# One kernel for a graph layer with attention and experts: edge totals by a running sum on VectorE, ranks between turned tiles, and the change behind the last step fetched earlier

## The reference, cut to what matters

```
xn = layernorm(x)
x  = x + gnn(xn, edges) + linear_attention(xn)
x  = x + experts(layernorm(x))
```

## Time and profile before

| | |
|---|---|
| median of 3 runs | 1640.06 us (1639.51 to 1644.37) |
| profiled execution | 1639.86 us |
| its span | 1637.8 us |
| TensorE busy | 1553.7 us |
| VectorE busy | 812.1 us |
| ScalarE busy | 335.5 us |
| GpSimd busy | 250.5 us |
| mean DMA rate | 100 GB/s |

### The profile page before, as it was taken

One profiled execution on the slowest core, in us unless ns is written; L12 is line 12 of the kernel. 1 busy time (PEld: TensorE's weight loads), 2 busy tenths in 40 slices (PEclk: granted clock), 3 DMA queues, 4 the chain that ended last, 5 costly groups with the idle time before them and its releaser, 6 DMA issues.

```text
span 1637.8 us, 21951 instructions
## 1 busy us (share of the span) xinstructions
PE 1553.7 (95%) x8501; PEld 1033.9 (63%) x8502; DVE 812.1 (50%) x1539; ACT 335.5 (20%) x493; POOL 250.5 (15%) x234
## 2 busy tenths in 40 slices
PE   6999999999899999999989999899999999999995
PEld 4566666557779999999887555444444444444442
DVE  7545447998877889994897333111111111111111
ACT  2321112001223245560372210100100000001000
POOL 1087820000000000000000027111111111111110
PEclk9999999999999999999989999999999999999998
DMA  9900010000004625313111327925629211613315
GB/s 273 334 2 1 2 61 1 1 1 1 1 1 116 159 82 172 67 33 84 32 47 59 145 54 154 332 66 195 221 54 322 91 48 53 211 44 122 135 30 193
DMA packets 85337, 163.79 MB, mean 100 GB/s; under 512 B 18874, under 2 KB 48816, under 8 KB 85001
## 3 DMA queue, kind: packets, MB, share of 16 engines
q1 hardware_dynamic: 66903, 119.07, 22.4%
q0 software_dynamic: 12096, 23.27, 6.2%
q10 hardware_dynamic: 6258, 20.40, 4.4%
HBM read 127.75 MB, written 37.56 MB: 101 GB/s over the span
## 4 chain that ended last, share of the span: by engine, by line
PE 65%; DVE 11%; POOL 8%; issue 6%; DMA 4%; SPq 3%; ACT 1%; DVEq 1%; POOLq 0%
PE bank L803 30%; PE bank L1629 7%; POOL slot_table L1312 7%; PE bank L1667 5%; PE bank L1531 5%; PE bank L1588 3%; PE bank L713 2%; DVE arena L2388 2%; DVE arena L2357 2%; SPq L372 2%; PE bank L1467 2%; PE bank L1414 2%; DMA expert_in<-arena 2%; PE bank L1715 1%; POOL expert_in L671 1%
## 5 line engine op out<-in xcount | busy, mean ns | idle before, releaser
L803 PE MATMUL bank<-arena 128*64 128x384 f32 x3312 | 539.7, 487 | 3.6 <-DMA arena<-in_L_ffn_w_down_dram 2.4
L803 PEld LDWEIGHTS bank<-arena 128*64 128x64 f32 x3312 | 236.7, 137 | 295.0 <-issue 290.2
L1156 DVE SCALAR_TENSOR_TENSOR arena<-bank,arena 64x384 f32<-64x384 f32 x88 | 50.3, 610 | 352.6 <-DMA arena<-out_dram,arena 198.3
L1667 PE MATMUL bank<-arena 125*125 125x198 f32 (+1 forms) x1200 | 192.4, 322 | 9.7 <-DVE arena L2357 9.6
L1667 PEld LDWEIGHTS bank<-arena 125*125 125x125 f32 x1200 | 186.2, 196 | 13.8 <-DVE arena L2357 13.7
L1629 PE MATMUL bank<-arena 128*125 128x192 f32 x960 | 163.2, 328 | 0.0
L1629 PEld LDWEIGHTS bank<-arena 128*125 128x125 f32 x960 | 157.7, 189 | 0.1
L1312 POOL DMA_INDIRECT slot_table<-arena x80 | 109.9, 1374 | 104.6 <-issue 104.6
L2194 DVE TENSOR_TENSOR arena<-arena,bank 125x417 f32 x186 | 109.5, 589 | 27.2 <-PE bank L1467 18.9
L664 POOL MEMSET arena<- 1x2500 f32 x1 | 2.2, 2177 | 599.0 <-DVE arena L2340 599.0
L2388 DVE SCALAR_TENSOR_TENSOR arena<-arena 125x1250 f32<-125x1250 f32 x60 | 91.1, 1519 | 4.4 <-ACT arena L1904 4.3
(11 more groups left out here) (307 smaller groups left out, 1570.7 us busy)
## 6 DMA issues: line engine op xcount, KB each, us to landing
arena<-in_L_ffn_w_gate_dram SPq DMA_DIRECT2D x9, 2304.0 KB, 9.0
arena<-in_L_ffn_w_up_dram SPq DMA_DIRECT2D x9, 2304.0 KB, 10.3
arena<-in_L_ffn_w_down_dram SPq DMA_DIRECT2D x9, 2304.0 KB
arena<-score_rows ACTq DMA_DIRECT2D x18, 585.9 KB
expert_in<-arena SPq DMA_DIRECT2D x23, 384.0 KB, 10.0
arena<-expert_in ACTq DMA_DIRECT2D x23, 384.0 KB, 3.3
arena<-in_L_mix_w_qkv_dram SPq DMA_DIRECT2D x2, 2304.0 KB, 17.4
xn_columns<-arena SPq DMA_DIRECT2D x1, 3750.0 KB, 14.9
```

Of the source, the lines that this page charges most:

```text
L803: ins = tp.matmul(ps[bank][HP * h:HP * h + HP, 0:384], frm[:, b, k, HP * h:HP * h + HP], ew[h][i][:, k, n * 384:(n + 1) * 384], start=(k = ...
L1667: ins = tp.matmul(ps[bank][0:T, c * width:(c + 1) * width], ptile[0:T, j % NPT, dt * T:(dt + 1) * T], values(n - first, st), start=(st == ...
```

## The change

The one-hots are laid out bucket by column. VectorE makes a running sum over the 160 columns within each bucket (`edges_up_to`, three scans of 10 buckets with a mask that is 0 at the first column of a bucket). The edge totals on TensorE, their copies and the bases are gone. The bucket counts are one product with the running sum's last column. A rank is the running sum over all partitions, minus the one-hots of this partition and those above it, plus the start: three products of 480 columns. TensorE works out ranks 0 to 5 between the turned tiles 4 to 9, ranks 6 to 9 in `edge_work(2)` and `edge_work(3)`, and `edge_slots` follows at g = 3. The counts and starts stand one and two key products later in TensorE's order.

For a change behind the last step, 2 is taken from its step, and its weights go to a space of their own (`SPARE`, where down follows gate in the same place). VectorE works out three places for each change in place of the half. SyncE waits for the output rows before the first change and not behind the last one.

```diff
-        later = small(EC, BF16)
-        onehot = take(EC * NBK, BF16).rearrange("p (c b) -> p c b", c=EC)
-        base0 = take(EC * NBK, BF16).rearrange("p (c b) -> p c b", c=EC)
+        BPART = 10
+        onehot_f = take(EC * NBK, BF16)
+        onehot = onehot_f.rearrange("p (b c) -> p b c", b=NBK)
+        upto_f = take(EC * NBK, BF16)
+        upto = upto_f.rearrange("p (b c) -> p b c", b=NBK)
+        notlower = take(P, BF16)
+        runmask = take(BPART * EC, BF16)
...
+        RE = NT - 4
...
+        SPARE = [SMALL + 2 * EWW, SMALL + 3 * EWW, SMALL + 2 * EWW]
...
             sp.wait_ge(s_et, 2)
+            sp.wait_ge(s_fout, 32 * NT)
             for c in range(NB1):
...
-                b = sp.value_load(change_i[0:1, 2, c:c + 1], min_val=0, max_val=1)
+                to = [sp.value_load(change_i[0:1, 2 + i, c:c + 1], min_val=0, max_val=ARENA - EWW) for i in range(3)]
                 for i, (w, done, each) in enumerate(((w_gate, s_g, 2), (w_up, s_up, 2), (w_down, s_y, 1))):
                     sp.wait_ge(s_ew[i], 16 * (c + 2))
+                    if i == 2:
+                        sp.wait_ge(s_ew[0], 16 * (c + 3))
                     sp.wait_ge(done, at_step * each + 1)
-                    sp.dma_start(arena[:, bass.ds(b * (EW[i][1] - EW[i][0]) + EW[i][0], EWW)].rearrange("p (k n) -> p k n", k=KD),
+                    sp.dma_start(arena[:, bass.ds(to[i], EWW)].rearrange("p (k n) -> p k n", k=KD),
...
-            sp.wait_ge(s_fout, 32 * NT)
...
+                step(dv.tensor_scalar(chu[0:1], cht[0:1], float(NTM), None, ALU.is_ge))
...
-                for v, what in enumerate((cht, che, isr)):
+                step(stt(out=cht[0:1], in0=chu[0:1], scalar=-2.0, in1=cht[0:1], op0=ALU.mult, op1=ALU.add))
+                for v in range(5):
+                    what = (cht, che)[v] if v < 2 else chc
+                    if v >= 2:
+                        to = EW[v - 2]
+                        step(dv.tensor_scalar(chc[0:1], isr[0:1], float(to[1] - to[0]), float(to[0]), ALU.mult, ALU.add))
+                        step.wait()
+                        step(stt(out=chc[0:1], in0=chu[0:1], scalar=float(SPARE[v - 2] - to[0]), in1=chc[0:1],
+                                 op0=ALU.mult, op1=ALU.add))
...
+            step(pl.memset(runmask, 1.0))
+            step.wait()
+            pl.memset(runmask.rearrange("p (b c) -> p b c", b=BPART)[:, :, 0:1], 0.0).then_inc(s_runmask, 1)
...
             def edge_counts():
-                pe.wait_ge(s_totc, 2)
-                tp.matmul(ps[6][0:NBK, 0:1], tot0[:, :], ones_b[:, 0:1], start=True, stop=False)
-                tp.matmul(ps[6][0:NBK, 0:1], tot1[0:EC1, :], ones_b[0:EC1, 0:1], start=False, stop=True).then_inc(s_cnt, 1)
+                pe.wait_ge(s_oh, 5)
+                pe.wait_ge(s_upto, NBK // BPART)
+                tp.matmul(ps[6][0:NBK, 0:1], upto[0:T, :, EC - 1], ones_b[0:T, 0:1], start=True, stop=True).then_inc(s_cnt, 1)
...
-                o = ps[6 + j % 2][0:T, 0:RC * NBK]
+                o = ps[6 + j % 2][0:T, 0:NBK * RC]
                 cs = slice(RC * j, RC * j + RC)
-                tp.matmul(o, tri[0:T, 0:T], onehot[0:T, cs, :], start=True, stop=False)
-                tp.matmul(o, ones_b[:, 0:T], base0[:, cs, :], start=False, stop=False)
...
+                tp.matmul(o, ones_b[0:T, 0:T], upto[0:T, :, cs], start=True, stop=False)
+                tp.matmul(o, notlower[0:T, 0:T], onehot[0:T, :, cs], start=False, stop=False)
+                tp.matmul(o, ones_b[0:1, 0:T], startrow[0:1, 0:NBK].unsqueeze(2).to_broadcast([1, NBK, RC]),
                           start=False, stop=True).then_inc(s_rank, 1)
...
             key_product(1, 0)
-            edge_totals()
             turn_x(2)
             turn_x(3)
+            key_product(2, 0)
+            key_product(0, 1)
             edge_counts()
-            key_product(2, 0)
+            key_product(1, 1)
             edge_starts()
-            key_product(0, 1)
-            key_product(1, 1)
             key_product(2, 1)
             for t in range(4, NT):
                 turn_x(t)
-            edge_work(1)
+                edge_rank(t - 4)
...
+            def edges_up_to(n):
+
+                part = slice(BPART * EC * n, BPART * EC * (n + 1))
+                if n == 0:
+                    dve.wait_ge(s_oh, 5)
+                    dve.wait_ge(s_runmask, 1)
+                dv.tensor_tensor_scan(upto_f[0:T, part], runmask[0:T], onehot_f[0:T, part], 0.0, ALU.mult, ALU.add)\
+                    .then_inc(s_upto, 1)
...
-                step(dv.tensor_reduce(rank[0:T, cs], rank_tmp[0:T, j % 2], AX.X, ALU.add))
+                step(dv.tensor_reduce(rank[0:T, cs], rank_tmp[0:T, j % 2].rearrange("p b c -> p c b"), AX.X, ALU.add))
...
             key_feature(0, 0)
+            edges_up_to(0)
             group_stats(2)
             key_feature(1, 0)
-            dve.wait_ge(s_tot, 1)
-            dv.tensor_copy(tot0, ps[4][:, 0:NBK]).then_inc(s_totc, 1)
-            dv.tensor_copy(tot1[0:EC1], ps[5][0:EC1, 0:NBK]).then_inc(s_totc, 1)
+            edges_up_to(1)
             group_stats(3)
-            bucket_chunks()
-            edge_bases()
+            edges_up_to(2)
             key_feature(2, 0)
             group_stats(4)
             ln_mean_var(2)
+            key_feature(0, 1)
+            bucket_chunks()
+            normalise_rows(2)
             bucket_starts()
-            key_feature(0, 1)
-            normalise_rows(2)
             key_feature(1, 1)
```

More of the change, by code:

```diff
@@ L209, in gps_layer @@
         rank = take(EC)
-        rank_tmp = take(960).rearrange("p (i c b) -> p i c b", i=2, c=16)
+        rank_tmp = take(960).rearrange("p (i b c) -> p i b c", i=2, c=16)
         RC = 16
         RJ = EC // RC
+        RE = NT - 4
+        assert RE + 4 == RJ
         TC = 8
@@ L358, in gps_layer @@
         stepw = route(NTM)
-        change_i = route(3 * NB1, I32).rearrange("p (v r) -> p v r", v=3)
+        chu = route(NB1)
+        change_i = route(5 * NB1, I32).rearrange("p (v r) -> p v r", v=5)
         loads_i = route(NTM, I32)
@@ L393, in gps_layer @@
         s_oh = sem("edge_onehot")
-        s_tot = sem("edge_totals")
-        s_totc = sem("edge_totals_copied")
-        s_br = sem("edge_base_ready")
+        s_runmask = sem("mask_of_running_sum")
+        s_upto = sem("edges_up_to_column")
         s_cnt = sem("bucket_counts")
@@ L1287, in _ @@
             step(pl.memset(triinc, 1.0))
-            step(pl.memset(later, 1.0))
+            step(pl.memset(notlower, -1.0))
             step.wait()
@@ L1297, in _ @@
                              pattern=[[1, P]], channel_multiplier=-1).then_inc(s_const, 1)
-            pl.affine_select(out=later, in_=later, compare_op=ALU.is_ge, fill=0.0, base=-1,
-                             pattern=[[1, EC]], channel_multiplier=-1).then_inc(s_const, 1)
+            pl.affine_select(out=notlower, in_=notlower, compare_op=ALU.is_ge, fill=0.0, base=0,
+                             pattern=[[-1, P]], channel_multiplier=1).then_inc(s_const, 1)
             pl.memset(zeros, 0.0).then_inc(s_const, 1)
             pool.wait_ge(s_const, 9)
+            step(pl.memset(runmask, 1.0))
+            step.wait()
+            pl.memset(runmask.rearrange("p (b c) -> p b c", b=BPART)[:, :, 0:1], 0.0).then_inc(s_runmask, 1)
             step(pl.iota(pad_info.bitcast(I32), pattern=[[1, 2 * NTM]], base=1 << 20, channel_multiplier=2 * NTM))
@@ L1321, in _ @@
             tp.transpose(ps[7][:, 0:38], rowsin[0:38, :], ident[0:38, 0:38]).then_inc(s_colps, 1)
[L1322 to L1325, removed]
-                for b in range(NBK):
-                    ins = tp.matmul(ps[5][0:EC1, b:b + 1], onehot[0:T, P:EC, b], ones_b[0:T, 0:1], start=True, stop=True)
-                ins.then_inc(s_tot, 1)
             def turn_x(t):
@@ L1385, in edge_work @@
             def edge_work(g):
-                if 1 <= g < 5:
-                    for j in range(3 * (g - 1), min(3 * g, RJ)):
+                if g in (2, 3):
+                    for j in range(RE + 2 * (g - 2), RE + 2 * (g - 1)):
                         edge_rank(j)
@@ L2013, in normalise_rows @@
                         .then_inc(s_xn, 1)
-            def edge_bases():
-                dve.wait_ge(s_totc, 2)
-                dv.tensor_tensor(base0, tot0.unsqueeze(1).to_broadcast([P, EC, NBK]),
-                                 later.unsqueeze(2).to_broadcast([P, EC, NBK]), ALU.mult).then_inc(s_br, 1)
-                dv.tensor_tensor(base1[0:EC1], tot1[0:EC1].unsqueeze(1).to_broadcast([EC1, EC1, NBK]),
-                                 tri[0:EC1, 0:EC1].unsqueeze(2).to_broadcast([EC1, EC1, NBK]), ALU.mult).then_inc(s_br, 1)
+            def edges_up_to(n):
[5 more added lines that the diff above has]
+                    .then_inc(s_upto, 1)
             def bucket_chunks():
@@ L2097, in edge_work @@
             def edge_work(g):
-                if 1 <= g < 5:
-                    for j in range(3 * (g - 1), min(3 * g, RJ)):
```

(7 more changed lines are left out.)

20 lines of the change are left out of this document (6 added, 14 removed).

## The result

| | before | changed |
|---|---|---|
| median of 4 runs each | 1642.21 us (1639.51 to 1645.67) | 1627.01 us (1624.42 to 1627.35) |
| ratio | | 0.991, 95% interval 0.9888 to 0.9932 |
| profiled execution, its span | 1639.86, 1637.8 us | 1627.27, 1625.5 us |

The kernel became 0.9% faster, 1.0 us above the forecast and inside the range. The profiled executions differ by 12.6 us, where the sum had 14.3. In span it is 12.3 us: the last scatter is issued 9.2 us earlier (1622.42 to 1613.18), and 3.1 us less lie behind it (15.4 to 12.3).

A forecast was written before the change was run, and what follows sets the result against it. TensorE, busy 95% of the span, was taken as the bound, with the slots' chain ending beside it at W1. 1639.86 less 11.3 (start) and 3.0 (end) made 1625.6, predicted as 1626 us, range 1621 to 1631.

The forecast's parts named there:

- TensorE's side: Start, TensorE's order: key product (3,1) starts at 71.1 instead of 78.57, 7.4 us earlier.
- Up to there nothing on it changes: TensorE's order until the two first key products end at 25.09 us: claimed unchanged.
- The scans: VectorE's three running sums at the start: 3.4 us each, ending at 37.2, so TensorE waits 1.8 us.
- rival of fast scans: VectorE's scans take 1.7 us each, no wait at the counts, total 1624; chance 0.12.
- The wait should not cost the clock: TensorE's 1.8 us wait for the scans at the bucket counts: claimed to leave the granted clock at 1.00.
- rival of the clock: TensorE's clock falls anyway, at 27 or at 221 us; total 1628.6; chance 0.10.
- Tiles with ranks: TensorE's tiles 4 to 9 with ranks 0 to 5: six times 0.83 plus 0.88, 10.3 us, to 55.5.
- The slots' side: Start, VectorE's slots and GpSimd's scatters: 10.6 us earlier, VectorE free for the turned W1 at 217.5.
- rival of the slow reduction: VectorE's rank reduction, reading words 64 bytes apart, doubles to 1.3 us; total 1627.5; chance 0.06.
- The hole at W1: TensorE's wait before W1 times W2 closes: start at 220.6, 9.3 us earlier, and 2 us more if clock holds.
- The end: Last weights fetched two steps sooner, so the last scatter lands in 2.9 us instead of 5.9: 3.0 us gained.
- The other side: TensorE reads the 20 rank products' moving operand slowly; at 1 us more each, total 1646; chance 0.05.

The follow-up runs named there:

- mask_late: Changed kernel with GpSimd filling the scans' mask only after VectorE's first one-hots; 1628.04 us (4 runs), ratio 0.9921 to the kernel before.
- mask_twice2: Changed kernel with GpSimd filling the scans' mask twice, one fill behind the other; 1626.35 us (one run).
- combo_w: combo with VectorE's rank product written column by bucket, so the reduction reads words side by side; 1623.91 us (6 runs), ratio 0.9897 to before.
- counts_later: Changed kernel with bucket counts behind key product (1,1) and starts behind (2,1); 1623.88 us (4 runs), ratio 0.9901 to before.
- combo: Changed kernel with both the later mask fill and the bucket counts and starts one key product later; 1623.79 us (6 runs), ratio 0.9901 to before.
- after_again: The changed kernel run once more, unedited; 1626.43 us (6 runs), ratio 0.9914 to before.
- one_sooner: Changed kernel with the last change of expert weights fetched one step sooner than before instead of two; 1628.04 us (one run).
- start_only: Kernel before with only the running sum and moved ranks, without the earlier weight fetch; 1631.25 us (6 runs), ratio 0.9948.
- tail_only: Kernel before with only the earlier fetch of the last weights into their own space; 1636.56 us (median of 10), ratio 0.9983.

## Why the prediction was right, and by how much its steps were off

Two rows of before, VectorE's and then GpSimd's, on which the first point below rests:

```profile
4.51 0.87 DVE L1954 CAST arena<-arena 125x320 f32<-125x320 int32 x1 [4.51 <-DMA arena<-in_dst_dram]
```

```profile
4.46 0.73 POOL L1300 MEMSET arena<- 128x768 f32 x1
```

**TensorE's side** was to come to the key product (3,1) at 71.1 and came at 73.06. Stretch by stretch, later or earlier than forecast:

| stretch | forecast | measured | off |
|---|---|---|---|
| end of the two first key products | 25.09 | 25.96 | +0.9 |
| tiles 2 and 3, to key product (2,0) | 27.5 | 28.23 | -0.1 |
| two key products and the wait, to the counts | 37.2 | 38.21 | +0.3 |
| counts, two key products, to tile 4 | 45.2 | 48.17 | +2.0 |
| tiles 4 to 9 with ranks 0 to 5 | 55.5 | 57.42 | -1.1 |
| on to key product (3,1) | 71.1 | 73.06 | 0.0 |

- *"Up to there nothing on it changes"* failed. I had costed the mask at nothing because GpSimd was idle; what it held was VectorE. `mask_late` and `mask_twice2` show it. The trace of before had the pattern in two rows that I passed over, of VectorE and of GpSimd: its first conversion ran beside a fill of 128x768 and took 0.87 us, the same form later 0.33. The hold is 1.2 us in the changed kernel against 0.5 before. With the edges that arrived 0.47 us later in this execution (4.98 for 4.51) it makes the 1.1 us by which the turning starts later (15.27 for 14.14). The Trainium skill ("SBUF — State Buffer", section "SBUF: two separate sides") says that VectorE in a mode with two ports and a GpSimd instruction share one pair of ports under an exclusive lock, so that the one that comes later waits for the other's end. Every held instruction here ended 0.17 to 0.19 us behind the end of a GpSimd fill (or, in `combo_w`, of a short index instruction), which agrees; in which mode the conversions run no row shows. One detail fits less well: in `counts_later` the conversion's row starts at 5.16, 0.03 us ahead of the fill's, and it was the conversion that waited.
- *The scans* were right: 3.48 us against 3.4, 2.17 ns an element, twice the 1.07 of the products of two tensors. The half throughput that the Trainium skill ("DVE: opcode table, instruction layouts, handler registers and perf-mode slots", section 6) gives the scan agrees with this, though no run here shows that the feedback is its reason. The rival of fast scans falls. The wait was 2.08 us against 1.8.
- *"The wait should not cost the clock"* was wrong: 1.7 us at the key product (5.82 for 4.13). This is the rival of the clock, at a place that I had excluded by a row from 1036 us. That row was one execution of another pattern. The fall hangs on the wait: in the three profiled executions without it (`counts_later`, `combo`, `combo_w`) the clock stayed at 1.00. But the wait doesn't always bring it: of the six with this wait of 2.08 us (changed kernel, `after_again`, `mask_late`, `one_sooner`, `start_only`, `mask_twice2`) the last two kept the clock. In these two the first 24 matmuls of the key products had taken 9.05 and 9.33 us, in the four others 8.03 to 8.76; whether that matters, nothing here tests.
- *Tiles with ranks* were 1.54 us a pair and not 1.71, because the work behind a tile starts 0.64 to 0.70 us after its first transpose: the 0.83 that I took is its duration with the modelled end. 6 x 0.17 = 1.0 us back.

**The slots' side** was to be 10.6 us earlier and was 7.8: the 1.8 us of rank 9, which TensorE ended at 68.8 and not 67.0, and 1.0 us because VectorE ends it 2.4 us later and not 1.4: 0.6 us for two reductions of 0.96, and some 0.4 because rank 8 was not as far as I had assumed. The rival of the slow reduction was right in kind and, at 0.3 us and not 0.65 each, half its size; VectorE begins a rank every 1.55 to 1.62 us against TensorE's 1.54, and in six ranks that brought TensorE no wait. `combo_w` shows that the layout is the cause, for writes as for reads; the penalty on crossing into another 16-byte line that the Trainium skill ("SBUF — State Buffer", section "Door 1") gives agrees with both. The scatters and the reading back gave away 0.7 us more, so VectorE copied the first piece of W1 at 220.95 and not 217.5.

**The hole at W1** closed as forecast in kind: both sides now arrive together (219.76 and 220.95), the clock held in this execution, and from W1 times W2 to VectorE's first count it is 3.49 us (222.82 to 226.31) instead of 5.68 (229.94 to 235.62), the 2 us that the forecast had for it. That was in part luck: the second half of the clock's rival, the fall at 221, came true in four of the nine profiled executions with the new start, where 1.3 to 1.7 of these 2 us were lost again. 7.1 and 2.2 make 9.3 us at the first count, where 11.3 were forecast; the 9.2 at the last scatter are the same, though between them single stages differ by 1 to 3 us from execution to execution (from the experts' first product to the last scatter 579.4 to 586.7 us over these kernels).

**The end** was right: 3.1 us against 3.0, alone 3.0 by the medians, and `start_only` keeps the old landing of 5.5. The 9.8 us behind the last landing stayed. **The list of changes and SyncE's wait** cost nothing that shows: the last scatter of `tail_only` is issued 1.2 us later than that of before, and 0.8 of it are there before the changed code. **The other side**, slow reads by TensorE, falls with 0.20, 0.30 and 0.34 us from one matmul of a rank to the next.

**The sum** in profiled executions: 9.2 + 3.1 = 12.3 us of span for 14.3. The 2.0 us are TensorE's 1.9 at W1 (219.76 for 217.9: the clock 1.7 and the later start 0.9 above all, less the 1.0 of the pairs) and some 0.4 because the slots' side was the later of the two there, less 0.2 and 0.1 by which the clock and the end gave more than forecast. That the median came within 1.0 us of the forecast owes something to the spread: by the medians beside each other it is 15.2 us, by the profiled executions 12.6, by the two parts run alone 11.4. It owes something to errors that cancel as well: the clock's 1.7 and the start's 0.9 against the 1.0 of the pairs. Three sums of the prediction are also slightly off, with no effect on the forecast: at 1.7 us each the scans end at 32.1 and not 32.3, slow reductions make 1628 and not 1627.5, and clock and tail together make 1631.6, just outside the range that they were to bound.

## What to carry to other kernels

An engine that is idle isn't free to work: look which instruction of another engine will run beside the new one, and whether a row of the same kind already shows it longer beside a fill. Work moved from TensorE to VectorE can come back as a wait in TensorE's order, and a wait costs its length and, at times, the clock behind it; so put the product that needs the result one large product later than the sum says. Two chains that end together must both be shortened, and the gain is that of the slower one.

## What the runs showed of the hardware

- Beside a GpSimd fill of 128x1600 bf16 (1.43 to 1.61 us) a VectorE conversion of 125x320 takes 1.51 to 1.64 us for 0.33: it ends 0.17 to 0.19 us after the fill. A fill of 128x768 f32 (0.73 us) does the same; row statistics on VectorE beside the larger fill kept their 1.93 us.
- The running sum took 3.48 us for 1600 bf16 elements.
- VectorE reading 480 f32 words 64 bytes apart: 0.96 us for 0.65; writing them 120 bytes apart: 1.05 for 0.66. TensorE reading 480 columns in runs of 32 bytes, 320 bytes apart: no more than in one run.
- The same wait of 2.08 us was followed by a fall of the granted clock in 4 executions of 6, with 5.82 us for the key product in all four and 4.12 us where the clock held. At W1 times W2 it fell in 4 of 9. What decides between them stays open.
- At the very start the granted clock reads 1.00, and yet the first 24 matmuls of the key products took from 8.03 us (changed kernel) to 9.66 us (`combo_w`). This too stays open.
